# Loading each expert block by transposing DMAs instead of a plain load and TensorE transposes, in a graph layer with a mixture of experts

## What is computed

```python
xn = _layernorm(x)
x = x + _L0_gnn_ref(xn, edges, ...) + _L0_mix_ref(xn[None], ...)[0]
x = x + _L0_ffn_ref(_layernorm(x)[None], ...)[0]

def _L0_ffn_ref(x, Wg, bg, bias, W1, b1, W2, b2):
    gate_logits = x_flat @ Wg + bg + bias
    topk_vals, topk_idx = jax.lax.top_k(gate_logits, 2)
    topk_w = jax.nn.softmax(topk_vals, axis=-1)
    combine = (one_hot(topk_idx, 8) * topk_w[..., None]).sum(axis=1)
    h = relu(einsum('td,edh->teh', x_flat, W1) + b1)
    y = einsum('teh,ehd->ted', h, W2) + b2
    out = einsum('ted,te->td', y, combine)
```

## Time and profile before

| | |
|---|---|
| median of 3 runs | 2495.51 us (2495.32 to 2496.86) |
| the profiled execution's own time | 2498.49 us |
| its span in the trace | 2496.9 us |
| TensorE busy over the span | 2178.9 us (87%), matmuls and transposes |
| VectorE busy | 1599.3 us (64%) |
| ScalarE busy | 1179.6 us (47%) |
| GpSimd busy | 370.7 us (15%) |
| mean granted TensorE clock | 0.913 of full speed |

### The profile page before, as it was taken

How to read it: one execution, slowest core, us unless ns; L and a number is a source line. 1 busy time by engine, 2 the same in 40 slices (tenths; PEclk the granted TensorE clock), 3 DMA queues, 4 the chain that set the end, 5 groups by cost and what they waited for, 6 DMA issues and landing times.

```text
span 2496.9 us, 53050 instructions
## 1 busy us (share of the span) xinstructions
PE 2178.9 (87%) x15108; PEld 1348.5 (54%) x15109; DVE 1599.3 (64%) x4782; ACT 1179.6 (47%) x2382; POOL 370.7 (15%) x431
## 2 busy tenths in 40 slices
PE   2655656599999999999899997999999997499997
PEld 1444444355655555555455553444444443389996
DVE  6999998688888888888232232344444445255554
ACT  2444443255555555555444443344444443266664
POOL 1000000100000000000111011121121212166665
PEclk9555566799999999999899998999999999699999
DMA  2111111022222222222221113555555553555563
GB/s 77 39 33 37 38 35 32 27 116 115 111 115 118 108 117 117 109 116 118 80 80 65 48 52 119 199 182 203 191 196 200 183 204 124 174 93 93 86 94 49
DMA packets 125110, 268.02 MB, mean 107 GB/s; under 512 B 30350, under 2 KB 78527, under 8 KB 122867
## 3 DMA queue, kind: packets, MB, share of 16 engines
q1 hardware_dynamic: 99043, 215.95, 24.7%
q0 software_dynamic: 26000, 51.27, 9.0%
HBM read 137.14 MB, written 131.87 MB: 108 GB/s over the span
## 4 chain that ended last, share of the span: by engine, by line
PE 64%; issue 15%; DVE 10%; DVEq 5%; POOLq 2%; POOL 1%; SPq 1%; DMA 1%; ACT 1%; ACTq 0%
PE bank L1959 42%; PE bank L1950 6%; PE bank L2154 6%; PE bank L2168 5%; POOLq L747 2%; DVE big L1002 2%; DVEq L1017 1%; DVE big L992 1%; DVEq L988 1%; DVEq L1001 1%; DVE big L999 1%; PE bank L2139 1%; DVE R L977 1%; PE bank L1967 1%; DVE R L970 0%
## 5 line engine op out<-in xcount | busy, mean ns | idle before, releaser
L1959 PE MATMUL bank<-RW,big 128*128 128x512 f16 (+1 forms) x4900 | 1180.5, 380 | 0.0
L1959 PEld LDWEIGHTS bank<-RW,big 128*128 128x128 f16 x4900 | 443.9, 98 | 396.4 <-issue 3.8
L1651 ACT ACTIVATE big<-bank 128x512 f16<-128x512 f32 (+1 forms) x640 | 372.0, 581 | 335.3 <-PE bank L1950 335.1
L1149 DVE TENSOR_TENSOR big<-iotaB,keys 128x512 f16<-128x512 f16 x1300 | 452.3, 418 | 7.9 <-issue 7.8
L1950 PE MATMUL bank<-big 128*128 128x128 f16 x2560 | 248.3, 219 | 12.0 <-DVE big L1149 11.8
L1950 PEld LDWEIGHTS bank<-big 128*128 128x128 f16 x2560 | 191.0, 98 | 123.8 <-DVE big L1149 12.5
L862 POOL DMA_INDIRECT out_dram<-big x112 | 178.7, 1595 | 146.2 <-ACT big L1788 108.8
L1778 ACT ACTIVATE big<-bank,b1A,iscA 128x256 f32<-128x256 f32 x224 | 114.1, 560 | 100.2 <-PE bank L2154 98.0
L2154 PE MATMUL bank<-big,RW 128*128 128x256 f16 x1344 | 157.6, 275 | 0.0
L2168 PE MATMUL bank<-RW,big 128*128 x1344 | 156.0, 273 | 0.3 <-DVE big L1529 0.2
L2154 PEld LDWEIGHTS bank<-big,RW 128*128 x1344 | 132.4, 99 | 16.3
(11 more groups left out here) (372 smaller groups left out, 2859.5 us busy)
## 6 DMA issues: line engine op xcount, KB each, us to landing
big<-a_dram SPq DMA_DIRECT2D x49, 832.0 KB
big<-a_dram SPq DMA_DIRECT2D x49, 768.0 KB, 4.5
a_dram<-big SPq DMA_DIRECT2D x49, 640.0 KB, 3.0
a_dram<-big SPq DMA_DIRECT2D x49, 512.0 KB, 2.6
a_dram<-big SPq DMA_DIRECT2D x49, 448.0 KB, 2.5
big<-rows_dram SPq DMA_DIRECT2D x56, 265.0 KB
big<-in_x_dram SPq DMA_DIRECT2D x96, 128.0 KB, 2.1
big<-in_L_ffn_W_dram POOLq DMA_DIRECT2D x16, 512.0 KB, 4.6
```

The costliest lines, as they stand in the source:

```text
L1149: last = v.tensor_tensor(out[q].rearrange("p b (m k) -> p b m k", k=2), inturn(iotaB[:, :], QB, P // 2), twice(kd[:, q * QB:(q + 1) * QB, ...
L1651: a.activation(Ab[q][:, 0:n], banks[BB(q)][:, 0:n], ACT.Copy).then_inc(s_ab, 1)
L1959: last = mm(bank[:, :], blk(q, c), src, start=(u == 0), stop=(u == T))
```

## The change

The plain load of a block is replaced by five DMAs on SP's queue: four transposing DMAs, each of 256 rows by 128 f16 columns of `rows_dram`, written to 128 partitions by 256 columns of `xt5`, the layout that `up5` reads, and one plain DMA for the 9 f32 numbers behind each row, straight into `gates`. `xt5` now has four buffers instead of two, and the raw buffers `xbr` are gone. `turned5` on TensorE and `turn5` on ScalarE are gone with their semaphores. `up5` and `leave5` wait for the five DMAs by `s_xb` (`LOADS` = 80 is five times 16). SP waits for `up5` of block b-4 before it overwrites a buffer. SP's blocks are written out instead of looped, so table places are constants, and the loops of TensorE and VectorE run over four blocks instead of two.

```diff
+LOADS = 5 * 16
...
-        xbr = [sp5.f16(2 * ROWW) for _ in range(2)]
...
-        xt5 = [sp5.f16(4 * BLK).rearrange("p (c n) -> p c n", c=4) for _ in range(2)]
+        xt5 = [sp5.f16(4 * BLK).rearrange("p (c n) -> p c n", c=4) for _ in range(4)]
...
-            def load5(b, par):
-                sp.wait_ge(s_xc, b + 1)
-                n = sp.value_load(needI[0:1, bass.ds(b, 1)], min_val=16, max_val=48)
-                r = sp.value_load(rowI[0:1, bass.ds(b, 1)], min_val=0, max_val=SPARE_ROW)
+            def load5(b):
+                n = sp.value_load(needI[0:1, b:b + 1], min_val=16, max_val=48)
+                r = sp.value_load(rowI[0:1, b:b + 1], min_val=0, max_val=SPARE_ROW)
                 sp.wait_ge(s_we, n)
-                sp.dma_start(xbr[par].bitcast(F32),
-                             rows_dram[bass.ds(r, BLK), :].rearrange("(p j) c -> p (j c)", j=2))\
-                  .then_inc(s_xb[par], 16)
-
...
+                if b >= 4:
+                    sp.wait_ge(s_up, 2 * (b - 4) + 6)
+                for c in range(4):
+                    sp.dma_start_transpose(out=xt5[b % 4][:, c, :],
+                                           in_=rows_dram.bitcast(F16)[bass.ds(r, BLK), c * P:(c + 1) * P])\
+                      .then_inc(s_xb[b % 4], 16)
+                sp.dma_start(gates[:, b * 2 * GATE:(b + 1) * 2 * GATE].rearrange("p (j n) -> p j n", j=2),
+                             rows_dram[bass.ds(r, BLK), D:D + GATE].rearrange("(j p) n -> p j n", j=2))\
+                  .then_inc(s_xb[b % 4], 16)
+
+            for b in range(NBLK):
+                load5(b)
...
-            def leave5(b, par, times):
+            def leave5(b, par, times, i4, need):
...
-                dve.wait_ge(s_xc, b + 3)
+                dve.wait_ge(s_xb[i4], need)
...
-            def turn5(b, par):
-                act.wait_ge(s_tx, b + 3)
-                act.wait_ge(s_up, b * 2 + 2)
-                a.activation(gates[:, bass.ds(b * (2 * GATE), 2 * GATE)].rearrange("p (j n) -> p j n", j=2), xbg[par], ACT.Copy)
-                a.activation(xt5[par].rearrange("p c n -> p (c n)"), bankh[4 + par][:, :], ACT.Copy).then_inc(s_xc, 1)
-
...
-            def turned5(b, par, half):
-
-                pe.wait_ge(s_xb[par], half * 16 + 16)
-                pe.wait_ge(s_xc, b + 1)
-                for c in range(4):
-                    for j in range(2):
-                        last = nc.tensor.transpose(bankh[4 + par][:, (2 * c + j) * P:(2 * c + j + 1) * P],
-                                                   xb5[par][:, j, c * P:(c + 1) * P], ident16[:, :])
-                last.then_inc(s_tx, 1)
-
-            def up5(b, par):
+            def up5(b, par, i4, need):
...
-                pe.wait_ge(s_xc, b + 3)
+                pe.wait_ge(s_xb[i4], need)
```

More of the change, by code:

```diff
@@ L347, in gps_layer @@
         sp5 = Space()
-        xbr = [sp5.f16(2 * ROWW) for _ in range(2)]
-        xb5 = [r.rearrange("p (j n) -> p j n", j=2) for r in xbr]
-        xbg = [r.bitcast(F32).rearrange("p (j n) -> p j n", j=2)[:, :, D:D + GATE] for r in xbr]
-        xt5 = [sp5.f16(4 * BLK).rearrange("p (c n) -> p c n", c=4) for _ in range(2)]
+        xt5 = [sp5.f16(4 * BLK).rearrange("p (c n) -> p c n", c=4) for _ in range(4)]
         h32 = [sp5.f32(4 * BLK) for _ in range(2)]
@@ L511, in gps_layer @@
         s_b2 = sem("s_b2")
-        s_xb = [sem(f"s_xb{i}") for i in range(2)]
-        s_tx = sem("s_tx")
-        s_xc = sem("s_xc")
+        s_xb = [sem(f"s_xb{i}") for i in range(4)]
         s_up = sem("s_up")
@@ L1551, in _ @@
             split5(0, 0)
[L1552 to L1561, removed]
+            for b in range(4):
+                split5(b + 1, (b + 1) % 2)
+                leave5(b, b % 2, b // 2, b, LOADS)
+            with dve.Fori(1, NBLK // 4 - 1) as k:
+                for i in range(4):
+                    split5(4 * k + i + 1, (i + 1) % 2)
+                    leave5(4 * k + i, i % 2, 2 * k + i // 2, i, LOADS * k + LOADS)
+            for b in range(NBLK - 4, NBLK):
+                if b < NBLK - 1:
+                    split5(b + 1, (b + 1) % 2)
+                leave5(b, b % 2, b // 2, b % 4, LOADS * (NBLK // 4))
         @block.scalar
@@ L1568, in _ @@
             for n, c in ((1, s_xlo), (4, s_ab), (2, s_ag[0]), (2, s_ag[1]),
-                         (4, s_hr), (1, s_yl), (4, s_ua), (2, s_xc), (2, s_yg)):
+                         (4, s_hr), (1, s_yl), (4, s_ua), (2, s_yg)):
                 a.activation(cred[:, 0:1], ones[:, 0:1], ACT.Copy).then_inc(c, n)
@@ L1789, in gate5 @@
                 last.then_inc(s_yg, 1)
-            turn5(0, 0)
-            turn5(1, 1)
             relu5(0, 0)
@@ L1795, in _ @@
                 relu5(b + 1, 1 - b)
-                turn5(b + 2, b)
                 if b:
@@ L1801, in _ @@
                     relu5(2 * k + par + 1, 1 - par)
-                    turn5(2 * k + par + 2, par)
                     gate5(2 * k + par - 1, 1 - par)
@@ L1813, in _ @@
             for n, c in ((1, s_xt), (Q, s_bl), (Q, s_ap[0]),
-                         (W, s_yp), (2, s_dp), (2, s_tx), (4, s_up)):
+                         (W, s_yp), (2, s_dp), (4, s_up)):
                 mm(banks[6][:, 0:P], zeros16[:, :], zeros16[:, :], start=True, stop=True).then_inc(c, n)
@@ L2153, in up5 @@
                         for wp, xp in ((0, 0), (0, 1), (1, 0)):
-                            last = mm(o, w1(e, wp, k, f), xt5[par][:, 2 * xp + k, :], start=(n == 0), stop=(n == 5))
+                            last = mm(o, w1(e, wp, k, f), xt5[i4][:, 2 * xp + k, :], start=(n == 0), stop=(n == 5))
                             n += 1
@@ L2172, in down5 @@
                 last.then_inc(s_dp, 1)
[L2174 to L2182, removed]
+            assert NBLK % 4 == 0
+            up5(0, 0, 0, LOADS)
+            with pe.Fori(0, NBLK // 4 - 1) as k:
+                for i in range(4):
+                    up5(4 * k + i + 1, (i + 1) % 2, (i + 1) % 4, LOADS * k + LOADS * ((i + 1) // 4 + 1))
+                    down5(4 * k + i, i % 2)
+            for b in range(NBLK - 4, NBLK - 2):
+                up5(b + 1, (b + 1) % 2, (b + 1) % 4, LOADS * ((b + 1) // 4 + 1))
+                down5(b, b % 2)
+            up5(NBLK - 1, 1, 3, LOADS * (NBLK // 4))
             down5(NBLK - 2, 0)
```

## The result

The changed kernel takes 2576.12 us (median of 4 runs, 2572.66 to 2579.78) against 2495.97 us before (4 runs), a ratio of 1.0315 with a 95% interval of 1.0298 to 1.0332. The profiled execution took 2572.66 us, the fastest of the four, with a span of 2571.1 us.

The account below looks back on a forecast made before the run. TensorE was taken to bound the kernel before, SP's queue after: 2152.9 us start + 369.6 us for 56 blocks + 26.4 us ending = 2548.9 us span, less 1.4 gives 2548 us median, 2.1% slower; range 2468 to 2610 us.

Parts of the forecast that it names:

- The step that carried it: Expert stage: SP's queue, issuing five DMAs a block, becomes the bound instead of TensorE, with a loss; chance 0.54.
- SP's beat: SP's queue time per block: 1.68 us plus four transposing issues of 1.23 us, 6.6 us against TensorE's 5.24.
- The hold p: Time for which one transposing DMA holds SP's queue, taken as 1.1 us; break-even at 0.87 us.
- landing, last products and tail: End of the stage after the last issue: 2.6 us landing, 7.9 us products, 15.9 us tail, together 26.4 us.
- a choice between rows: Issue cost on SP's queue set nearer POOL's plain scatter, 0.99 us for 128 rows, than SP's plain DMA, 0.333 us.
- The argument by the work on the pieces: On SP's queue, rows spread over 128 partitions need block-by-block setup, so a transposing issue costs a little above 0.99 us.
- All hidden: SP's issues stay hidden below 0.76 us each; TensorE bounds at 5.24 us a block, 2471 us; chance 0.28.
- The way out to the scatters: From gate5 through the scatters, 8.65 us per two blocks must fit 10.48 us; scatters may land 1.8 us later.
- The DMA engines: Loads cost 2.7 us a block at 32 ns a packet; as bound, 12.0 us and about 2850 us; chance 0.05.
- The clock rival: TensorE's clock falls in the gaps; half the work at half speed gives 7.9 us a block, near 2620 us; chance 0.07.

Follow-up runs that it names:

- e1_one: One transposing DMA a block (256 rows by 512 columns) instead of the changed kernel's four; 2476.12 us, 0.9906 of the kernel before.
- e4_plain: One plain, untransposed DMA of the same 256 x 512 numbers instead of the changed kernel's four transposing ones; 2472.75 us, 0.9886 of the kernel before.
- e3_eight: Eight transposing DMAs a block, each 128 rows by 128 columns, instead of the changed kernel's four; 2869.3 us in one run.
- e2_two: Two transposing DMAs a block, each 256 rows by 256 columns, instead of the changed kernel's four; 2481.0 us, 0.9917 of the kernel before.
- e7_one_pe: Changed kernel with one transposing DMA a block, plus eight idle transposes on TensorE behind each up5; 2496.81 us, 1.0004 of the kernel before.

## Why the prediction came out as it did

**The step that carried it held.** SP's queue became the bound, and TensorE is idle 1.4 us a block by the windows ((50 - 40.14) us over 50 / 7.03 blocks), 1.2 us of it at `up5`, as written. The range of 2468 to 2610 us holds 2576 us, and the direction is right. The loss was put too low: 52 us were predicted and 80 measured.

**What was mis-sized is SP's beat**, 7.03 us where 6.6 was predicted. The hold p came out at 1.154 us against 1.1, which is 0.22 us a block. The rest, 7.03 - 4 x (1.154 + 0.13) = 1.89 us against 1.68, is 0.21 us: the gate DMA takes 0.43 us instead of the 0.35 of the plain load, the gap ahead of it is 0.20 us instead of 0.13 (2304.07, where the last transposing DMA ends, to 2304.27), and the instruction that waits on `s_up`, though it has nothing to wait for, takes some 0.06 us with its gap. Over 56 blocks the two together make 24.1 us. The other terms of the sum are small: the stage began 3.0 us earlier (2149.9; its start lies anywhere from there to 2157.6 in the profiles of the experiments, which have the same code ahead of it), and landing, last products and tail took 2571.1 - (2149.9 + 393.7) = 27.5 us against 26.4. The tail did not get shorter with slower blocks as I had argued: from TensorE's end at 2554.4 to the end pass 16.7 us, the same as before. Together 2548.9 + 24.1 - 3.0 + 1.1 = 2571.1 us, the measured span. The last 6 us are that I put the median 1.4 us below the span, as it was before, while this time the profiled execution was the fastest of four and the median lies 5.0 us above its span.

**The value of p was a choice between rows**. It is near POOL's plain scatter (0.99 us), but it doesn't grow with the rows as I argued: 128 rows by 128 columns hold 1.15 us, 256 by 128 1.15, 256 by 256 1.20, 256 by 512 1.25. The argument by the work on the pieces was wrong, and that the number it led to was nearly right was luck: the choice of the slower rows decided between a gain and a loss, and nothing in the trace before could show it. What the choice got right is only that a transposing DMA is dearer to issue than a plain one. Why a transposing DMA holds the queue so long, at nearly every size, no run shows.

**The rivals.** "All hidden" needed p below 0.76 us for four instructions; its time of 2471 us, 0.990 of before, is what the kernel gives when the instructions are fewer (0.9906 in e1_one, 0.9886 with the plain load of e4_plain), so its gain was sized well and its condition was not met. The way out to the scatters, with its 8.65 us for two blocks, was no obstacle at 5.24 us a block. The Trainium skill says that transposing DMAs are as fast as regular ones ("Advanced Engine Details and Errata", "X-Bar Transpose (TRN2)"). Of the issue that does not hold here: one holds the queue 1.15 to 1.28 us against 0.33 to 0.43 us for a plain one. In the work of the DMA engines it nearly holds, as the lines of SP's DMAs in 2200 to 2450 us show (packets, MB, share of 16 engines), e1_one first and e4_plain second:

```profile
q1 hardware_dynamic: 59083, 12.05, 30.4%
q1 hardware_dynamic: 24403, 12.14, 24.2%
```

In both 44 blocks were loaded in this window, so a block costs 1.7 us of all 16 engines transposed and 1.4 us plain, a quarter more. TensorE is the bound in both kernels, so their times do not show this difference.

**The DMA engines** came out cheaper than predicted. In 2200 to 2450 us the changed kernel shows (packets, MB, share of 16 engines):

```profile
q0 software_dynamic: 10269, 8.87, 30.3%
q1 hardware_dynamic: 50825, 9.69, 23.4%
```

That is 936 us of engine time over 50825 packets, 18 ns each instead of the 32 ns taken from the earlier trace rows, and 1.6 us a block instead of 2.7. The clock rival didn't occur in the steady part of the changed kernel: 1.00 with gaps of 1.4 us a block. Twice, near the start and near the end, TensorE waited longer at `up5` (start us, us, what, and in brackets the wait ahead of it):

```profile
2180.62 4.46 PE L2133 MATMUL bank<-big,RW 128*128 128x256 f16 x24 [2.38 <-DMA big<-rows_dram]
2539.12 4.46 PE L2133 MATMUL bank<-big,RW 128*128 128x256 f16 x24 [3.08 <-DMA big<-rows_dram]
```

The trace shows the granted clock at 0.5, 1.2 GHz, for 3.4 us during each of these, and the 24 products took 4.46 us instead of 2.8. That is 1.7 us of TensorE's time at each place, small beside the loss of 80 us.

## What to carry to other kernels

When work moves from an engine to DMAs, count the instructions on the issuing queue before the bytes: here four instructions of 1.29 us each, on top of 1.9 us for the table reads and the plain DMA, overran a beat of 5.24 us, and the same bytes in one instruction turned a loss of 3.15% into a gain of 0.94%. A queue that waits 190 us in the profile has slack per block only, so divide it by the number of blocks (3.4 us here) before giving it three or four more issues. And when an engine is idle in every window while no other is full, look for the queue that feeds it in the chain.

## What the runs showed of the hardware

- A transposing DMA of f16 from memory, issued on SP's queue, holds that queue 1.15 us for 128 x 128 and 256 x 128 numbers (e3_eight, the changed kernel), 1.20 for 256 x 256 (e2_two) and 1.25 to 1.28 for 256 x 512 (e1_one, e7_one_pe). The same queue takes 0.37 us for a plain DMA of 256 x 512 (e4_plain).
- On the DMA engines a transposing load of a block with its gate numbers took 1.7 us of all 16 (30.4% of 250 us over 44 blocks in e1_one), against 1.4 us for the plain one of e4_plain (24.2%) and 1.0 us for the plain load of whole rows before (18.0%).
- The granted clock stayed at 1.00 with gaps of 1.4 us in blocks of 7.0 us, fell to 0.5 for 3.4 us after single waits of 2.38 and 3.08 us, and averaged 0.76 to 0.80 with blocks of 12.2 us and waits of some 5 us.
